# A recommendation tower on one core: layer 2 and layer 1 moved between the lookups, and one half turned by TensorE

## The reference

```python
e = jnp.stack([tbl_0[ids[:, 0]], ..., tbl_26[ids[:, 26]]], axis=1)   # 2048 x 27 x 128
interactions = jnp.einsum('bnd,bmd->bnm', e, e)                      # upper triangle: 351
h = jnp.concatenate([z, dense_ctx], axis=1)                          # 367
h = jnp.maximum(h @ W_top1 + b_top1, 0.0)                            # 512
h = jnp.maximum(h @ W_top2 + b_top2, 0.0)                            # 256
y = h @ W_top3                                                       # 1
```

## Time and profile before

| | |
|---|---|
| median of 3 runs | 386.87 us (386.56 to 387.27) |
| the profiled execution | 388.18 us, of which the span is 386.4 |
| busy, share of the span | PE 88%, DVE 66%, POOL 61%, ACT 53% |
| mean granted clock of TensorE in the span | 0.968 of full |
| moved by DMA | 67.10 MB, 174 GB/s |

### The profile page before, as it was taken

One profiled execution on the slowest core, in us unless ns is written; L12 is line 12 of the kernel. 1 busy time (PEld: TensorE's weight loads), 2 busy tenths in 40 slices (PEclk: granted clock), 3 DMA queues, 4 the chain that ended last, 5 costly groups with the idle time before them and its releaser, 6 DMA issues.

```text
span 386.4 us, 8058 instructions
## 1 busy us (share of the span) xinstructions
PE 340.0 (88%) x3338; PEld 276.0 (71%) x3338; DVE 256.2 (66%) x208; ACT 204.0 (53%) x300; POOL 235.3 (61%) x255
## 2 busy tenths in 40 slices
PE   2999899989995899989998998899987898848966
PEld 1767788658873688658975896578864688837965
DVE  6899995997187374998189727993497971620101
ACT  4898856444771367343774376236743236722631
POOL 6777777777777747776577777775772075720000
PEclk9999999999999899999999999999999699986989
DMA  7976955986659878977488869974899074773240
GB/s 173 227 168 164 275 136 171 252 240 173 165 49 216 203 247 134 250 234 203 116 172 224 238 178 162 237 219 152 186 242 212 3 196 137 146 194 119 48 80 6
DMA packets 70511, 67.10 MB, mean 174 GB/s; under 512 B 42522, under 2 KB 57447, under 8 KB 70475
## 3 DMA queue, kind: packets, MB, share of 16 engines
q1 hardware_dynamic: 59691, 50.10, 48.5%
q0 software_dynamic: 7936, 16.27, 21.3%
q10 hardware_dynamic: 2848, 0.23, 0.5%
HBM read 48.47 MB, written 18.10 MB: 172 GB/s over the span
## 4 chain that ended last, share of the span: by engine, by line
PE 50%; DMA 13%; DVE 10%; issue 10%; POOL 9%; SPq 7%; ACT 1%; ACTq 0%; DVEq 0%
PE gram_ps L707 12%; PE emb_ps L677 10%; PE mlp_ps L724 9%; PE emb_ps L679 9%; POOL rows L645 9%; DVE onehot L850 8%; PE mlp_ps L733 4%; DMA h<-tbl_rows 4%; SPq L479 4%; DMA products<-gram 4%; DMA rows<-tbl_rows,idx 2%; PE emb_ps L688 2%; DMA z<-products 2%; DVE flips L905 2%; PE emb_ps L751 1%
## 5 line engine op out<-in xcount | busy, mean ns | idle before, releaser
L645 POOL DMA_INDIRECT rows<-tbl_rows,idx x248 | 234.5, 946 | 104.6 <-issue 72.5
L850 DVE TENSOR_TENSOR onehot<-ids_b,row_id 125x2048 fp32r<-125x2048 int32 x76 | 168.8, 2273 | 41.8 <-PE emb_ps L679 33.5
L677 PE MATMUL emb_ps<-onehot,table_hi 125*128 125x512 f32 (+1 forms) x416 | 158.3, 390 | 27.0 <-DVE onehot L850 20.0
L679 PE MATMUL emb_ps<-onehot,table_lo 125*128 125x512 f32 (+1 forms) x416 | 152.2, 375 | 0.0
L677 PEld LDWEIGHTS emb_ps<-onehot,table_hi 125*128 125x128 f32 x416 | 80.7, 194 | 59.8 <-ACT emb L985 16.5
L679 PEld LDWEIGHTS emb_ps<-onehot,table_lo 125*128 125x128 f32 x416 | 80.8, 194 | 12.0
L707 PEld LDWEIGHTS gram_ps<-emb 128*54 128x54 f32 x2048 | 53.8, 130 | 7.6 <-issue 6.5
L707 PE MATMUL gram_ps<-emb 128*54 128x54 f32 x2048 | 56.0, 214 | 2.4 <-issue 1.6
L1016 ACT COPY emb<-moved 128x1024 f32<-128x1024 f32 (+1 forms) x21 | 42.3, 2016 | 21.6 <-DMA moved<-halves 21.3
L984 ACT COPY held<-emb_ps 128x256 f32<-128x256 f32 x40 | 15.0, 376 | 69.2 <-PE emb_ps L679 69.0
L1045 ACT COPY gram<-gram_ps 118x432 f32<-118x432 f32 x64 | 33.2, 519 | 29.6 <-PE gram_ps L707 28.6
(11 more groups left out here) (53 smaller groups left out, 132.2 us busy)
## 6 DMA issues: line engine op xcount, KB each, us to landing
halves<-flips SPq DMA_DIRECT2D x21, 512.0 KB, 4.2
moved<-halves SPq DMA_DIRECT2D x84, 128.0 KB
ids_b<-ids_onehot SPq DMA_DIRECT2D x33, 256.0 KB, 6.1
products<-gram SPq DMA_DIRECT2D x28, 216.0 KB, 5.5
gram<-tbl_rows SPq DMA_DIRECT2D x9, 480.0 KB
rows<-tbl_rows,idx POOLq DMA_INDIRECT x248
h<-tbl_rows SPq DMA_DIRECT2D x4, 480.0 KB
z<-products SPq DMA_DIRECT2D x14, 126.0 KB
```

The costliest lines, as they stand in the source:

```text
L645: pool.indirect_dma_start(out=rows[:, bank_number(p, t, n) % ROW_BANKS, f - first, :], out_offset=None, in_=gathered_tables[f], in_offset= ...
L677: nc.tensor.matmul(ps[:, 0:width], table_hi[0:ROWS, table, j, :], columns[:, c, :], start=j == 0, stop=False)
L679: last = nc.tensor.matmul(ps[:, 0:width], table_lo[0:ROWS, table, j, :], columns[:, c, :], start=False, stop=j == ROWS_PER - 1)
L850: nc.vector.tensor_tensor(onehot[0:ROWS, seq % ONEHOT_RING, 0:own * width].rearrange("p (j b) -> p j b", b=width), *operands, ALU.is_equal ...
```

## The change

Six things change.

- TensorE: layer 2 of pair p - 2 runs in cycle p, right behind the first lookup (before: at the end of cycle p - 1); for the last pairs it stays between the grams. Chunks 0 and 1 of layer 1 run in front of the last lookup, 2 and 3 behind it. In cycles 1 to 6 the turns (turn_second) come in front of both grams.
- ScalarE follows: the second half is taken behind the last lookup but one, the third half between the last lookup and chunks 2 and 3 of layer 1, and then come the turned banks and both tiles' take_gram. In cycle 7 the order is gram, third half, turned banks, gram.
- VectorE: the scores of p - 2 stand with the second half's flip before piece 5 (cycle 7: piece 4), and the third half's flip before piece 10, or behind the last piece where there are no more than ten.
- The third half of pair 6, (6,1,0), is no longer flipped: TensorE turns all four banks of tile 1 there (is_flipped).
- Both late tables are loaded in cycle 6, the first when layer 2 of pair 4 has read h1; before, the first was loaded at the end of cycle 5. The rounds stand before lookups 2 and 4, the splits before pieces 7 and 11.
- SyncE: store_products stands ahead of store_half(p,0,1), load_z ahead of load_half(p,0,1); one of the cycle's own ids is loaded at the cycle's start instead of two, three of the next cycle's before the third half's store instead of two, and store_y goes one cycle later and in front of these.

```diff
-    return p > 0 and (t == 0 or n < HALF_BANKS)
+    return p > 0 and (t == 0 or n < HALF_BANKS and p != LATE_PAIR)
...
-PIECES_BEFORE_FLIP = [0] + [8] * (PAIRS - 3) + [14, 6]
-LATE_SPLITS = [6, 10]
-HALF_AFTER = 4
-LATE_ROUNDS = [1, 3]
+PIECES_BEFORE_SCORE = [0] + [5] * (PAIRS - 2) + [4]
+PIECES_BEFORE_FLIP = 10
+LATE_SPLITS = [7, 11]
+LATE_ROUNDS = [2, 4]
...
SyncE
-                for i in ids[0:2]:
+                for i in ids[0:1]:
                     load_ids(i)
+                store_products(p - 1)
+                if p == LATE_PAIR:
+                    load_late_table(0)
                 store_half(p, 0, 1)
-                store_products(p - 1)
+                load_z(p - 1)
                 load_half(p, 0, 1)
                 if p == LATE_PAIR:
                     load_late_table(1)
-                load_z(p - 1)
                 load_dense(p)
-                for i in ids[2:]:
+                for i in ids[1:]:
                     load_ids(i)
-                for i in ahead[0:2]:
+                if p >= 2:
+                    store_y(p - 2)
+                for i in ahead[0:3]:
                     load_ids(i)
-                store_half(p, 1, 0)
-                for i in ahead[2:3]:
-                    load_ids(i)
-                load_half(p, 1, 0)
+                if (p, 1, 0) in HALF_NUMBER:
+                    store_half(p, 1, 0)
+                    load_half(p, 1, 0)
...
TensorE
+                looks = len(cycle_lookups(p))
+                for at in range(looks - 1):
+                    look_ahead(p, at)
+                    if at == 0 and p > 1:
+                        layer2(p - 2)
...
+                for m in range(M1):
+                    if m == M1 // 2:
+                        look_ahead(p, looks - 1)
+                    layer1(p - 1, m)
+                if p < LAST:
+                    turn_second(p)
+                    gram_products(p, 0)
+                    gram_products(p, 1)
+                else:
+                    gram_products(p, 0)
                     layer2(p - 1)
-                gram_products(p, 1)
+                    turn_second(p)
+                    gram_products(p, 1)
...
VectorE
-                    if at == ONEHOT_RING + 1:
+                    if at == PIECES_BEFORE_SCORE[p]:
+                        if p >= 2:
+                            for t in range(TILES):
+                                score(p - 2, t)
                         flip_half(p, 0, 1)
-                    elif at == PIECES_BEFORE_FLIP[p]:
+                    elif at == PIECES_BEFORE_FLIP and (p, 1, 0) in HALF_NUMBER:
                         flip_half(p, 1, 0)
...
ScalarE
+                take_half(p, 0, 1)
...
+                for m in range(M1 // 2):
+                    take_layer1(chunk, m)
+                take_ahead(p, looks - 1)
+                if p < LAST:
+                    if (p, 1, 0) in HALF_NUMBER:
+                        take_half(p, 1, 0)
+                    for m in range(M1 // 2, M1):
                         take_layer1(chunk, m)
-                if p == 0:
-
-                    act.wait_ge(table_split, NO * GRAM_BANKS)
-                take_gram(p, 0)
-                if p < LAST:
+                    take_second(p)
+                    take_gram(p, 0)
                     place_dense(p)
-                if p > 0:
-                    for n in range(HALF_BANKS, TURN_BANKS):
-                        take_turned(p, 1, n)
+                    take_gram(p, 1)
```

More of the change, by code:

```diff
@@ L164, in list_banks @@
         if p > 0:
-            out += [("turn", p * TILES + 1, n) for n in range(HALF_BANKS, TURN_BANKS)]
+            out += [("turn", p * TILES + 1, n) for n in range(TURN_BANKS) if not is_flipped(p, 1, n)]
     return out
@@ L790, in _, with look_ahead @@
                 spread_ids(k)
[L791 to L803, removed]
-                if p > 0:
[L805 to L814, removed]
-                    for n in range(HALF_BANKS, TURN_BANKS):
-                        turn(p, 1, n)
+            def look_ahead(p, at):
+                for t, n in turns_ahead(p, at):
+                    turn(p, t, n)
+                i = cycle_lookups(p)[at]
+                for k in shared_ahead(i):
+                    spread_shared(k)
+                look_up(i)
+                if i + len(spread_ps) < NO:
+                    spread_ids(i + len(spread_ps))
+                elif i == NO - 2:
+                    spread_rows()
@@ new lines, in turn_second @@
+            def turn_second(p):
+                for n in range(TURN_BANKS):
+                    if not is_flipped(p, 1, n):
+                        turn(p, 1, n)
+            for at in range(NO):
+                look_ahead(0, at)
+            gram_products(0, 0)
+            gram_products(0, 1)
+            for p in range(1, PAIRS):
+                looks = len(cycle_lookups(p))
[3 more added lines that the diff above has]
+                        layer2(p - 2)
+                if p == 1:
+                    pe.wait_ge(weights_loaded, 2 * 16)
+                    pe.wait_ge(rows_placed, 1)
+                pe.wait_ge(z_loaded, p * Z_LOADS * 16)
+                for m in range(M1):
[8 more added lines that the diff above has]
+                    gram_products(p, 0)
@@ L934, in _ @@
                     make_onehot(i, part)
-                if PIECES_BEFORE_FLIP[p] >= len(pieces):
+                if len(pieces) <= PIECES_BEFORE_FLIP and (p, 1, 0) in HALF_NUMBER:
                     flip_half(p, 1, 0)
@@ L1080, in _, with take_ahead, take_second @@
                     finish_onehot(0)
-            for p in range(PAIRS):
+            def take_ahead(p, at):
+                i = cycle_lookups(p)[at]
+                for t, n in turns_ahead(p, at):
+                    take_turned(p, t, n)
+                for k in shared_ahead(i):
+                    if k > 0:
+                        finish_onehot(k)
+                take_lookup(i)
+                if i == NO - 2:
+                    act.wait_ge(rows_spread, 1)
+                    nc.scalar.copy(rows23[:, :, :].rearrange("p n h -> p (n h)"), rows_ps[:, :]
+                                   ).then_inc(rows_placed, 1)
+                if i + 2 < NO:
+                    show_table(i + 2)
+                if i + ahead < NO:
+                    round_table(i + ahead)
+            def take_second(p):
+                for n in range(TURN_BANKS):
+                    if not is_flipped(p, 1, n):
+                        take_turned(p, 1, n)
+            for at in range(NO):
+                take_ahead(0, at)
+            act.wait_ge(table_split, NO * GRAM_BANKS)
+            take_gram(0, 0)
+            place_dense(0)
+            take_gram(0, 1)
+            for p in range(1, PAIRS):
+                looks, chunk = len(cycle_lookups(p)), (p - 1) * MLP_CHUNKS
                 if p == 2:
@@ L1084, in _ @@
                 place_held(p)
[L1085 to L1089, removed]
+                take_half(p, 0, 0)
+                for at in range(looks - 1):
                     if p == LATE_PAIR and at in LATE_ROUNDS:
                         round_late(LATE_ROUNDS.index(at))
[L1092 to L1096, removed]
[L1097 to L1106 removed]
@@ L1123, in _ @@
                     take_half(p, 1, 0)
-                take_gram(p, 1)
+                    take_second(p)
+                    take_gram(p, 1)
             act.wait_ge(gram_taken, PAIRS * PAIR_GRAMS)
```

31 lines of the change are left out of this document (8 added, 23 removed).

## The result

The changed kernel takes 406.95 us (median of 3 runs, 403.54 to 408.26) against 386.87: a ratio of 1.050, 95% interval 1.040 to 1.060. It is slower, by 20.1 us where 9.5 were forecast, and lies just above the range, which ended at 406. The profiled execution is one of 406.95 us with a span of 405.1, to set against a forecast span of 386.4 + 9.5 = 395.9.

A forecast was written before the change was run, and what follows sets the result against it. VectorE's one-hot pieces were taken to bound the lookups while it idles in the rest of the cycle. Cycles 1 to 5 +8.5, cycle 6 -3.5 and cycle 7 +4.5 made +9.5 us: 396.4 us, range 390 to 402, widened to 379 to 406.

The forecast's parts named there:

- The loop's terms: Cycles 1 to 5: VectorE's walk, third half's store, loads, ScalarE's takes and six gram banks close each cycle; +8.5 us.
- start of the store, after the cycle's: VectorE ends the third half's flip at t = 22.0, 20.1 in cycle 1; the store's issue takes 0.1 us more.
- the store: Third half's 512 KB to DRAM: 4.7 us with six lookups, 3.7 with five, between 2.9 quiet and 6.9 behind id loads.
- issue and landing of the four loads: Third half's loads in cycles 1 to 5: 1.75 us to issue, then 3.8 to land, bounded by 2.7 and 5.9.
- take_half to the third gram bank: ScalarE in cycles 1 to 5: take_half 2.05, two layer 1 takes 0.95, take_second 1.25, first take_gram 0.6 us.
- last six banks, with the clock: Six gram banks in cycles 1 to 5, 5.15 us, plus 1.7 us of clock loss, 2.5 after longer waits.
- Cycle 6: Late tables and ids come at cycle 6's start, third half turned: 50.8 us against 54.25, -3.5 (from -6 to -1).
- Cycle 7: z lands at about 19.6 again, with more work behind it: +4.5 us (from +2.7 to +6.5).
- the three terms of the forecast: Last pair, behind z: last lookup's ids 1 to 2 us late, that lookup 1.9 inside layer 1, take_second 0.9 uncovered.
- A: Relief wins in cycles 1 to 5: halves land in quiet times, TensorE itself ends long cycles; -15 us, 372; chance 0.22.
- B: Halves in cycles 1 to 5 as late as forecast, but TensorE's clock holds: 386.5 us, no change; chance 0.16.
- C: SyncE's queue falls behind, next first half late, store meets id loads: 2 us more in six cycles, 408; chance 0.16.

The follow-up runs named there:

- the early half: Changed kernel with the third half flipped before piece 8, stored and loaded ahead of the next pair's ids, pair 6's third half flipped again: 381.77 us, 0.986.
- the later take: Changed kernel, but ScalarE copies the third half behind the first gram tile's four copies in cycles 1 to 5: 395.02 us, 1.018 against the kernel before.
- layer 2 put back: Changed kernel with the third half copied behind the first tile's gram copies, and layer 2 of p - 1 between the gram tiles again: 388.69 us, 1.005.
- the second execution: The changed kernel run once more, unaltered, on the experiments' chip: 404.43 us, 1.048 against the kernel before.

## Why the prediction was right in direction and too small

The mechanism is the forecast's: the only long TensorE wait of cycles 1 to 5 outside cycle 2's z sits in the first gram tile, is released by take_gram, and has ScalarE waiting for moved just ahead of it; the clock falls behind it, and the lookups run with one gap above 1 us (1.13, in cycle 1). The loop's terms, summed over cycles 1 to 5 (predicted, then measured from the rows above and the same rows of the other cycles):

| term | predicted | measured |
|---|---|---|
| start of the store, after the cycle's | 109.0 | 111.3 |
| the store | 24.3 | 39.3 |
| issue and landing of the four loads | 27.8 | 26.5 |
| take_half to the third gram bank | 24.3 | 20.9 |
| last six banks, with the clock | 35.9 | 34.7 |

**The failed step is the store:** "With six lookups an id load is issued 1.3 us ahead of it, held by piece 9, so I take 4.7". It measured 8.8, 11.3 and 8.1 in cycles 1, 3 and 5, and 8.1 where 6.5 stood for cycle 2: 15.0 us more in all, against 11.4 by which the five cycles exceed the forecast. I had weighed one id load between a quiet row of 2.9 and a crowded one of 6.9; what counts is all that the queue still holds, in cycle 1 four loads, and the upper row was no upper bound. The quiet row was also the wrong one to take: it is the store of a second half, at t = 5.7. The third half's own store, issued before the change right behind two id loads, was never quiet. Its DMA issues in cycles 1 to 5 of the kernel before:

```profile
halves<-flips SPq DMA_DIRECT2D x1, 512.0 KB, 5.9
halves<-flips SPq DMA_DIRECT2D x1, 512.0 KB, 6.9
halves<-flips SPq DMA_DIRECT2D x1, 512.0 KB, 6.6
halves<-flips SPq DMA_DIRECT2D x1, 512.0 KB, 5.9
halves<-flips SPq DMA_DIRECT2D x1, 512.0 KB, 6.9
```

That is 32.2 us where 24.3 were taken, so these rows, already there, would have put 8 us more into the sum, and the change sends three id loads ahead instead of two. Cycle 4's 3.7, argued from an id load that "can go much earlier", measured 2.9, and the kernel with no id load ahead gave 3.8 to 4.4 in the six-lookup cycles. The Trainium skill (DMA: Bandwidth & Descriptors, section Two DMAs through the same engine are not ordered) says that within one queue of one DMA engine the descriptors start in order; the 1.54 MB moved before cycle 1's 0.52 MB store landed agree. The estimate of 3.2 us a transfer that the prediction weighed against its rows is given by the Trainium skill (DMA: Bandwidth & Descriptors, section Anatomy of one DMA) for the path of DMAs issued from GpSimd; of the five stores, which SyncE issued, only cycle 4's is near it.

**The other terms of cycles 1 to 5 held.** The third flip was done at t = 20.1 in cycle 1 and 21.8 in 3, 4 and 5 (20.1 and 22.0 predicted). In cycle 2 its store came 2.9 us late, since z, for which SyncE's queue waits, was issued at t = 18.8. A landing of 3.8 was about right (2.7 to 4.0). For the clock I took 10.1 us; the last six banks lost 34.7 - 5 x 5.15 = 8.9. Cycle 5 is 1.7 above its 44.0, cycle 3 is 6.6 above it, and cycle 4, at 41.66, is just under the 42 that I had named, because its store was quick. Together the four other terms came out 3.6 us below the forecast, which hid part of the store's 15.0.

**Cycle 6** was predicted 3.8 us too long, which hid another part. Both late tables and the first late ids came sooner: the ids' piece began at t = 21.9, not 24.5, and TensorE ended 47.0 us after the start. **Cycle 7** came out at the forecast sum (+4.6 for +4.5), in part by luck: z came at t = 20.9 instead of 19.6, and what follows z took 25.8 us against 22.5 before, 3.3 more, with the three terms of the forecast (late ids 1.6, the lookup, take_second 0.9) partly offset by a better granted clock (0.94 behind z against 0.86). Its first half is flipped at t = -0.7, behind a row bank that GpSimd could not reuse until it was turned, and the kernel that flips pair 6's third half again gets those 4.4 us back. **The last layers** took 1.9 us longer, where nothing was forecast; that part is between 13.3 us (at a granted clock of 1.00) and 18.4 us (at 0.78) long in the profiles of the experiments, and I give it no cause.

**The rivals.** A, the relief, did not come about, but it exists: where the store lands in 4 us the six-lookup cycles last 40 to 41 us, and the early half beats the kernel before. B is refuted: the clock fell, and holding it up brought about a third of the loss back. C had the time (408) and one of its reasons, the store meeting id loads, in four cycles of five, but priced it at 2 us a cycle where it was up to 6.6; its other reason, a late first half of the next pair, did not show (ScalarE takes it at t = 3.2 to 6.8 in cycles 2 to 6, before at 3.4 to 6.7). Its time is nearer than its reasons.

**What the prediction did not see** is that layer 2 between the grams had been cover for a copy that stands between them. This is no part of the miss in size: in the changed kernel the copy stands ahead of both grams, and there a half in time needs no such cover (no wait over 1 us in cycles 1, 3 and 5 with no id load ahead). It decides what a repair is worth: with the copy between the tiles 3.3 us of TensorE work have to stand beside it, as the later take (395.0) and layer 2 put back (388.7) show.

## What to carry to other kernels

Before moving work out of a gap, list what hides beneath it: a stretch that fills one engine may be the cover of a copy on another. Price a transfer by the bytes still waiting in its queue when it is issued, not by the one instruction ahead of it, and by rows of that same transfer before those of a quieter one; a load that is needed a cycle later belongs behind a store that is needed now. And where an in-order engine serves both an early and a late consumer, the order of a few short instructions decides: here 9 us from one copy of 2 us.

## What the runs showed of the hardware

An unexpected stretch lies in cycle 3 of the changed kernel. The windows of 2 us from 174 us on (DMA share and GB/s last):

```profile
174.00:176.00 2.00, 1.81 (x9) 1.21 (x8) 2.00 (x2) 0.97 (x2) 1.11 (x2) 1.00 0.86 227
176.00:178.00 2.00, 1.98 (x9) 1.33 (x8) 2.00 (x3) 0.00 (x0) 0.08 (x1) 1.00 0.15 10
178.00:180.00 2.00, 2.00 (x11) 1.68 (x10) 2.00 (x2) 0.76 (x3) 1.70 (x2) 1.00 0.02 8
180.00:182.00 2.00, 2.00 (x11) 1.74 (x10) 2.00 (x2) 2.00 (x3) 1.39 (x3) 1.00 0.25 98
182.00:184.00 2.00, 2.00 (x11) 1.65 (x10) 2.00 (x2) 0.72 (x2) 1.54 (x2) 1.00 0.68 195
```

For about 4 us the DMA engines moved 8 to 10 GB/s instead of some 200, with id loads issued and, from 178 us on, the store and a row gather too. The same place in the second execution fell to 46 and 26 GB/s. Cycle 3's store, issued at 178.27, falls into it and is the longest. No run here tells what holds the engines, nor why, with no id load ahead, cycle 4's store still takes 5.4 us with its queue otherwise empty; both stay open.
